# A post-norm decoder layer on one core: the self-attention scores in 64-row tiles, queries masked four ways out of PSUM, and every engine's order laid anew

## The chip, the core and the metric

The kernel runs on one core of a Trainium2 chip. A core has a matrix engine (TensorE, PE in the profile; its weight loads are PEld), a vector engine (VectorE, DVE), a scalar engine (ScalarE, ACT), GpSimd (POOL) and SyncE (SP), whose queue issues the DMAs. The engines run their own instruction streams in order and meet at semaphores. SBUF is the on-chip memory of 128 partitions. PSUM takes TensorE's results; here it is cut into six banks B0 to B5 of 512 columns and a double one, S.

The metric is the time of one execution on the device, in microseconds. The kernel before took 1192.78 us (median of three runs, 1187.5 to 1199.39).

## The reference, cut to what matters

128 sequences of 64 tokens, 128 features. Each of three blocks is followed by a residual sum and a layer norm.

```python
# 1: causal self-attention, 16 heads of 8; no softmax but a polynomial
att = einsum('bhid,bhjd->bhij', q, k) / sqrt(8), causal
p   = polymax(att)          # x > 0: x**2 + 1;  -100 <= x <= 0: 1 - x/100;  else 0;  all / 1000
x   = layernorm(x + (p @ v) @ W_proj)
# 2: cross-attention over 64 context rows, 16 heads of 64, softmax
x   = layernorm(x + softmax(q @ k.T / 8) @ v @ WO + bO)
# 3: 16 experts, the top 6 of a softmax router, gates normalised
x   = layernorm(x + sum_e gate_e * (x @ expert_w[e]) / sum(gate))
```

All in float32. Where the kernel multiplies with the faster float32r form, it splits a number into a high and a low part and adds three products (hi.hi, hi.lo, lo.hi): `mm3` in the code.

## The kernel before, in words

A tile is four sequences (`NB`), 256 tokens; there are 32 tiles. One **turn** of the main loop works on five tiles at once, a stage on each: `s1` (self-attention scores, tile i+2), `l1` (the rest of self-attention, and the context products Z and VB, tile i+1), `l2` (cross-attention, router logits, tile i), `ff` (gates and experts, tile i-1), `out` (last norm and store, tile i-2). There is one turn for each of the 32 tiles besides a few that fill and empty the pipeline; 30 or so run with all stages on.

What sets the order is written out in tables: `JOBS` is TensorE's order with the PSUM bank of each job, and `SP_ORDER`, `ACT_ORDER`, `DVE_ORDER`, `POOL_ORDER` are those of the other engines. Each word names a function (`row_max0` is `row_max(0)`). A job waits until its bank's last job was emptied.

The steps that the change and the prediction touch:

- **Q and K** (TensorE): 128x256 products into one bank each. Keys: ScalarE writes `kp_hi` (`move_keys`), VectorE `kp_lo` (`keys_lo0`, `keys_lo1`), masked two ways (even and odd heads). Queries: ScalarE moves Q to `q_sb` (step `Q`), GpSimd splits it (`q_hi`, `q_lo`), ScalarE masks the high part eight ways (`queries_hi0` and `queries_hi1`, four copies each, into `qm_hi`), VectorE the low part in one instruction of 2048 columns (L820, `queries_lo`).
- **S1_0 to S1_3** (TensorE): for a sequence, 128 contraction rows, 512 query columns (8 masks x 64 tokens), three products, one bank.
- **Polymax**: for each S1 bank ScalarE does `relu` and `square`, VectorE `allow` (L730), `pieces` (L736) and `p1_` (L741). Of these only `p1_` has both inputs in SBUF (`poly` and `allowed`).
- **Cross-attention**: S2 -> `row_max`, `less_max` (VectorE) -> `exp` (ScalarE) -> `row_sum`, `row_inv` (VectorE) -> `shares` (GpSimd, L890, 128x1024) -> the transposes PT -> AC.
- **Layer norms** 1, 2, 3 (`stats`, `var`, `eps` on VectorE, `root` on GpSimd, L885, `norm` on VectorE, L698, two instructions each with SBUF input and output).
- **Gates**: `gate0` to `gate19`, twenty small VectorE steps in a chain. **Experts**: FF0 to FF7 -> `weigh0` to `weigh7` (VectorE, L754) -> `add0.0` to `add1.4` (GpSimd, L904 and L909; the first of each five is 128x1024).
- **SyncE**: loads, the store, and `place0`, `place1`: four DMAs each of 256 KB that move `vb_raw` to `vb` (L352).

Of the kernel before, what the change touches and what calls it, by code (L numbers as in the profile page):

```python
# [1010 lines left out]
```

## Time and profile before

| | value |
|---|---|
| median of three runs | 1192.78 us |
| lowest, highest run | 1187.5, 1199.39 us |
| profiled execution, first to last instruction (its own time is not printed beside it) | 1184.6 us |
| busy: PE, DVE, ACT, POOL | 95%, 94%, 65%, 62% |
| granted TensorE clock, mean | 0.990 of full speed |
| DMA, mean | 78 GB/s; queue q1 30.7% of 16 engines |
| chain that ended last | PE 46%, DVE 33%, issue 17% |

Busy time is the union of an engine's records. A record of VectorE runs some tens of ns into the next one, so the time that an instruction takes of its engine is read from start to start. Matmul records overlap more: their starts, not their lengths, say how fast TensorE goes. A record's length includes the time in which an instruction that has started is held up.

### The profile page before, as it was taken

The numbers are of one execution on the slowest core, as the hardware profiler recorded it, in microseconds if no ns is written. First come the engines' busy times: TensorE is split into PE (matmuls) and PEld (weight loads), VectorE is DVE, ScalarE is ACT, GpSimd is POOL, SyncE is SP. The second block draws the span as 40 slices with busy tenths as digits, with TensorE's granted clock in tenths as the row PEclk, the third lists the DMA queues.
The fourth block names the chain that finished last, engine by engine and source line by source line (L and its number), as shares of the span: only waits on it lengthen the run. The fifth ranks groups of instructions, "written<-read, shape, count | busy, mean of one in ns | idle before, by whom it ended". The sixth has DMA issues, their size and how long they took to land.

```text
span 1184.6 us, 30898 instructions
## 1 busy us (share of the span) xinstructions
PE 1126.7 (95%) x9472; PEld 867.1 (73%) x9472; DVE 1112.7 (94%) x2699; ACT 770.0 (65%) x1578; POOL 736.9 (62%) x776
## 2 busy tenths in 40 slices
...
DMA packets 49998, 92.09 MB, mean 78 GB/s; under 512 B 6576, under 2 KB 28592, under 8 KB 49968
## 3 DMA queue, kind: packets, MB, share of 16 engines
q1 hardware_dynamic: 49968, 91.70, 30.7%
...
## 4 chain that ended last, share of the span: by engine, by line
PE 46%; DVE 33%; issue 17%; DVEq 1%; POOL 1%; ACT 1%; DMA 1%; SPq 0%; POOLq 0%
PE ps_B L368 36%; DVE weighted L754 7%; PE ps_S L368 5%; PE ps_B L476 5%; DVE x L698 5%; DVE p L741 3%; DVE allowed L730 3%; DVE rowmax L709 3%; DVE kp_lo L826 2%; DVE poly L736 2%; DVE stats L676 2%; DVE r L839 1%; DVE mv L682 1%; DVEq L246 1%; DVE rowsum L718 0%
## 5 line engine op out<-in xcount | busy, mean ns | idle before, releaser
L904 POOL TENSOR_TENSOR weighted<-weighted 128x1024 f32<-128x1024 f32 (+3 forms) x256 | 313.3, 1224 | 103.5 <-DVE weighted L754 100.5
L890 POOL TENSOR_TENSOR p<-p,rowinv 128x1024 f32<-128x1024 f32 x64 | 122.9, 1920 | 194.3 <-DVE rowinv L722 194.3
L542 ACT ACTIVATE z<-ps_B 128x512 f32<-128x512 f32 x256 | 149.7, 599 | 118.2 <-PE ps_B L368 115.3
L754 DVE TENSOR_TENSOR weighted<-ps_B,gate 128x512 f32<-128x512 f32 x256 | 171.8, 684 | 14.7 <-PE ps_B L368 9.5
L368 PE MATMUL ps_B<-cT_hi,a_hi 128*128 128x256 f32 x512 | 156.0, 305 | 1.5
L698 DVE TENSOR_SCALAR x<-r,mv,rstd 128x128 f32<-128x128 f32 x192 | 152.5, 835 | 2.9 <-POOL rstd L885 2.9
L542 ACT ACTIVATE vb_raw<-ps_B 128x512 f32<-128x512 f32 x256 | 147.4, 590 | 5.4 <-PE ps_B L368 3.0
L368 PE MATMUL ps_B<-cT_hi,a_lo 128*128 128x256 f32 x512 | 144.6, 282 | 0.0
L368 PE MATMUL ps_B<-cT_lo,a_hi 128*128 128x256 f32 x512 | 144.6, 282 | 0.0
L368 PE MATMUL ps_B<-vo_hi,cT_hi 128*128 128x512 f32 x256 | 112.7, 440 | 16.4 <-DVE kp_lo L826 10.5
L368 PEld LDWEIGHTS ps_B<-vb,p2T 128*64 128x64 f32 x2048 | 110.6, 137 | 23.4 <-issue 23.2
L368 PE MATMUL ps_S<-z,x1T 128*64 128x512 f32 x512 | 124.0, 605 | 2.6 <-DVE p L713 2.6
L368 PE MATMUL ps_B<-vb,p2T 128*64 128x128 f32 x2048 | 126.0, 276 | 0.0
L542 ACT ACTIVATE p2T<-ps_B 128x512 f32<-128x512 f32 x128 | 69.6, 595 | 75.1 <-PE ps_B L476 75.1
L885 POOL TENSOR_TENSOR rstd<-rstd,power 128x2 f32<-128x2 f32 x96 | 67.0, 708 | 82.2 <-DVE rstd L686 81.9
L368 PE MATMUL ps_B<-ex_hi,x2T_hi 128*128 128x512 f32 x256 | 110.5, 432 | 5.9 <-DVE weighted L754 3.6
L368 PEld LDWEIGHTS ps_B<-cT_hi,a_hi 128*128 128x128 f32 x512 | 97.1, 190 | 21.9 <-DVE r L839 13.9
L542 ACT ACTIVATE qm_hi<-q_hi,const 128x256 fp32r<-128x256 f32 x256 | 108.9, 499 | 5.7 <-POOL q_hi L932 5.5
L368 PE MATMUL ps_B<-ex_lo,x2T_hi 128*128 128x512 f32 x256 | 101.7, 397 | 0.0
L368 PE MATMUL ps_B<-ex_hi,x2T_lo 128*128 128x512 f32 x256 | 101.6, 397 | 0.0
L368 PE MATMUL ps_B<-vo_lo,cT_hi 128*128 128x512 f32 x256 | 100.7, 394 | 0.0
L730 DVE SCALAR_TENSOR_TENSOR allowed<-ps_B,const 128x512 f32<-128x512 f32 x128 | 87.0, 679 | 14.6 <-ACT relu L566 14.5
...
## 6 DMA issues: line engine op xcount, KB each, us to landing
vb<-vb_raw SPq DMA_DIRECT2D x256, 256.0 KB, 4.3
...
```

Of the source, the lines that this page charges most:

```text
L368: return pe.matmul(o, l, r, start=start, stop=stop)
L476: last = pe.transpose(ps[BANK[f"PT{r}" + "ab"[q]]][:, P * k:P * k + P], p2[:, r, P * j:P * j + P], ident)
L542: return nc.scalar.activation(dst, src, ACT.Copy, scale=scale)
L676: V.bn_stats(stats[:, n - 1, r], src[:, r]).then_inc(ln_stats[n - 1], 1)
L698: V.tensor_scalar(dst[:, r], src[:, r], mv[:, n - 1, r, 0:1], rstd[:, n - 1, r:r + 1], ALU.subtract, ALU.mult).then_inc(done, 1)
L709: V.tensor_reduce(rowmax[:, r], ps["S"][:].rearrange("p (h k) -> p h k", h=H), AX.X, ALU.max).then_inc(rowmax_ready, 1)
L730: V.scalar_tensor_tensor(allowed[:].rearrange("p (j n) -> p j n", j=J), ps[BANK[f"S1_{b}"]][:].rearrange("p (j n) -> p j n", j=J), -100.0, ...
L741: V.scalar_tensor_tensor(p1[:, b], poly[:], 1.0, allowed[:], ALU.add, ALU.mult).then_inc(p1_ready, 1)
L754: V.tensor_tensor(weighted[:, r, 512 * q:512 * q + 512].rearrange("p (e c) -> p e c", e=4), ps[BANK[job]][:].rearrange("p (e c) -> p e c", ...
L885: G.tensor_tensor(rstd[:, n - 1], rstd[:, n - 1], power[:], ALU.pow).then_inc(ln_rstd[n - 1], 1)
L890: G.tensor_tensor(weights, weights, rowinv[:, r].unsqueeze(2).broadcast_to([P, H, T]), ALU.mult).then_inc(p2_ready, 1)
L904: G.tensor_tensor(a, a, b, ALU.add).then_inc(add_steps, 1)
```

## The change

1. **Scores in two 64-row tiles.** Queries are masked four ways rather than eight (`NV = 4`), each mask keeping the heads of one 16-row group in either half of the partitions. A product takes 64 rows of keys (rows 0 to 63 or 64 to 127) against 256 query columns, and two such go to two banks, one after the other in the instruction stream. An S1 bank now holds four head pairs of two sequences instead of eight of one; S1_0 is issued with S1_1, S1_2 with S1_3, at the later one's place. `p1_` writes two blocks of 256 columns.
2. **Queries out of PSUM.** ScalarE writes `qm_hi` straight from Q's bank in four masked copies (`queries_hi`; the scale is in `query_mask`), VectorE writes `qm_lo` in four instructions of 256 columns from the same bank. Gone are the move to `q_sb`, GpSimd's `q_hi` and `q_lo`, four masked copies on ScalarE and the 2048-column instruction on VectorE.
3. **Orders.** All five tables are new. The setup products stand at their ends.

```diff
+PARTS = 2
+NV = J // PARTS
+PART = P // PARTS
...
 SP_ORDER = """
-    x_columns place0 store context x_rows place1
+    context x_rows x_columns store place0 place1
...
+    gate18 allow3 pieces3 attended gate19 stats2 weigh1 var2 weigh0 eps2 weigh3 weigh2 norm2 weigh7 weigh5 weigh4
+    logits p1_3 gate0 weigh6 gate1 product_lo0 product_lo1 product_lo2 product_lo3 product_lo4 product_lo5
...
+    context_hi context_lo add1.0 add1.1 add1.2 add1.3 add1.4 shares0 next_x_hi root3 shares1 root1 next_x_lo bias_x1
+    root2 add0.0 add0.1 x2_hi add0.2 x2_lo add0.3 add0.4 experts_hi experts_lo
...
+def latest(jobs, waited=()):
+
+    order = [job for job, _, _ in JOBS]
+    return [job for job in jobs if BANK[job] not in waited and job == last_of(order, [other for other in jobs if BANK[other] == BANK[job]])]
...
-                def s1(b):
-                    pe.wait_ge(qm_hi_ready, 2 * (u + 1))
-                    pe.wait_ge(qm_lo_ready, u + 1)
-                    wait_emptied(pe, i, "K")
-                    k_hi, k_lo = (a[:, b].rearrange("p a t -> p (a t)") for a in (kp_hi, kp_lo))
-                    q_hi, q_lo = (a[:, b].rearrange("p j t -> p (j t)") for a in (qm_hi, qm_lo))
-                    return mm3(ps[BANK[f"S1_{b}"]][:], k_hi, k_lo, q_hi, q_lo)
+                def s1(last_unit):
+                    units = range(last_unit - PARTS + 1, last_unit + 1)
+                    for job in latest(("Q", "K"), [BANK[f"S1_{unit}"] for unit in units]):
+                        wait_emptied(pe, i, job)
+                    seqs = range(NB * units[0] // 4, NB * (last_unit + 1) // 4)
+                    for s, b in enumerate(seqs):
+                        for n, (keys, queries) in enumerate(((kp_hi, qm_hi), (kp_hi, qm_lo), (kp_lo, qm_hi))):
+                            for g, unit in enumerate(units):
+                                rows = slice(PART * g, PART * g + PART)
+                                done = mm(ps[BANK[f"S1_{unit}"]][:, NV * T * s:NV * T * s + NV * T], keys[rows, b].rearrange("p a t -> p (a t)"),
+                                          queries[rows, b].rearrange("p v t -> p (v t)"), n == 0, n == 2)
...
-                def move_q():
-                    move("Q", q_sb[:], ps[BANK["Q"]][:, 0:TOK], float(HD) ** -0.5)
-
-                def queries_hi(half):
-
-                    act.wait_ge(q_hi_ready, u + 1)
-                    for j in range(4 * half, 4 * half + 4):
-                        last = copy(qm_hi[:, :, j], q_hi[:].rearrange("p (b t) -> p b t", b=NB), qmask[:, j:j + 1])
+                def queries_hi():
+
+                    wait_full(act, i, "Q")
+                    for v in range(NV):
+                        last = copy(qm_hi[:, :, v], ps[BANK["Q"]][:, 0:TOK].rearrange("p (b t) -> p b t", b=NB), query_mask[:, v:v + 1])
...
                 def p1_of(b):
...
-                    V.scalar_tensor_tensor(p1[:, b], poly[:], 1.0, allowed[:], ALU.add, ALU.mult).then_inc(p1_ready, 1)
+                    seqs, heads = slice(b // 2 * 2, b // 2 * 2 + 2), slice(b % 2 * NV * T, b % 2 * NV * T + NV * T)
+                    V.scalar_tensor_tensor(p1[:, seqs, heads], poly[:].rearrange("p (s n) -> p s n", s=2), 1.0, allowed[:].rearrange("p (s n) -> p s n", s=2), ALU.add, ALU.mult).then_inc(p1_ready, 1)
...
                 def queries_lo():
...
-                    dve.wait_ge(q_lo_ready, u + 1)
-                    V.tensor_tensor(qm_lo[:], q_lo[:].rearrange("p (b t) -> p b t", b=NB).unsqueeze(2).broadcast_to([P, NB, J, T]),
-                                    qmask.unsqueeze(1).unsqueeze(3).broadcast_to([P, NB, J, T]), ALU.mult).then_inc(qm_lo_ready, 1)
+                    dve.wait_ge(qm_hi_ready, u + 1)
+                    if isinstance(i, int) and u == 0:
+                        dve.wait_ge(mask_steps, 2)
+                    for v in range(NV):
+                        last = V.scalar_tensor_tensor(qm_lo[:, :, v], ps[BANK["Q"]][:, 0:TOK].rearrange("p (b t) -> p b t", b=NB), query_mask[:, v:v + 1],
+                                                      qm_hi[:, :, v].bitcast(F32), ALU.mult, ALU.subtract)
+                    last.then_inc(emptied[BANK["Q"]], 1)
...
-                def queries_hi():
-                    wait_emptied(pool, i, "Q")
-                    G.tensor_tensor(q_hi[:].bitcast(F32R), q_sb[:], one[:].broadcast_to([P, TOK]), ALU.mult).then_inc(q_hi_ready, 1)
-
-                def queries_lo():
-                    pool.wait_ge(q_hi_ready, u + 1)
-                    G.tensor_tensor(q_lo[:], q_sb[:], q_hi[:], ALU.subtract).then_inc(q_lo_ready, 1)
```

Three places of the new order, as the instruction streams have them. The first is VectorE in the loop, around the reciprocal `rowinv` of sequences 2 and 3 (`row_inv1`), which lets GpSimd start `shares1`. Before:

```order
L246 REGISTER_ALU [waits allowed_ready]
L741 SCALAR_TENSOR_TENSOR p1<-poly,allowed 128x512 [waits emptied_B1]
L722 RECIPROCAL rowinv<-rowsum 128x16 [waits rowsum_ready]
L763 REGISTER_ALU
L794 TENSOR_SCALAR tsum<-tsum 128x2 [waits gate_steps]
L763 REGISTER_ALU
L796 TENSOR_TENSOR gate<-prob,left 128x32 [waits gate_steps]
L679 REGISTER_ALU
L661 MEMSET scratch 128x1 [waits ln1_stats]
L682 BN_AGGR mv<-stats 128x2 x2
L729 REGISTER_ALU [waits p1_ready]
L730 SCALAR_TENSOR_TENSOR allowed<-ps_B4,const 128x512 [waits relu_ready]
```

And now:

```order
L812 TENSOR_TENSOR gate<-prob,left 128x32 [waits gate_steps]
L737 RECIPROCAL rowinv<-rowsum 128x16 [waits rowsum_ready]
L779 REGISTER_ALU
L814 RECIPROCAL tinv<-tsum 128x2 [waits gate_steps]
L252 ISA [waits allowed_ready]
L757 SCALAR_TENSOR_TENSOR p1<-poly,allowed 128x2x256 [waits emptied_B2]
L779 REGISTER_ALU
L816 TENSOR_TENSOR gate<-gate,tinv 128x32 [waits gate_steps]
L701 TENSOR_SCALAR rstd<-mv 128x2 [waits ln1_var]
L779 REGISTER_ALU
L818 TENSOR_REDUCE gsum<-gate 128x2 [waits gate_steps]
L252 ISA
```

Behind `rowinv` stood a small gate step, the statistics of a norm and `allowed`, which reads PSUM; now `p1` (two SBUF inputs), a gate product and the sum of norm 1 (`rstd<-mv`) stand there, and norms 3 and 1 follow within a few rows.

The second is GpSimd at the same place. Before:

```order
L888 REGISTER_ALU
L890 TENSOR_TENSOR p2<-p2,rowinv 128x1024 [waits rowinv_ready]
L870 TENSOR_TENSOR xT_lo<-xT,xT_hi 128x256 [waits xT_hi_ready]
L900 REGISTER_ALU
L904 TENSOR_TENSOR weighted<-weighted 128x128 [waits add_steps]
L885 TENSOR_TENSOR rstd<-rstd,power 128x2 [waits ln1_eps]
```

And now:

```order
L905 TENSOR_TENSOR rstd<-rstd,power 128x2 [waits ln3_eps]
L908 REGISTER_ALU
L910 TENSOR_TENSOR p2<-p2,rowinv 128x1024 [waits rowinv_ready]
L905 TENSOR_TENSOR rstd<-rstd,power 128x2 [waits ln1_eps]
L890 TENSOR_TENSOR xT_lo<-xT,xT_hi 128x256 [waits xT_hi_ready]
L969 REGISTER_ALU
L252 ISA [waits x1_ready]
```

`shares1` (`p2<-p2,rowinv`) now has norm 1's root and the split of the next x directly behind it.

The third is TensorE at S1_2 and S1_3. Before, S1_2 is three products of 512 columns into one bank, between Z and AC1:

```order
L368 MATMUL ps_B5<-cT_hi,a_hi 128x256
L368 MATMUL ps_B5<-cT_lo,a_hi 128x256
L368 MATMUL ps_B5<-cT_hi,a_lo 128x256
L246 REGISTER_ALU
L368 MATMUL ps_B3<-qm_hi,kp_hi 128x512
L368 MATMUL ps_B3<-qm_lo,kp_hi 128x512
L368 MATMUL ps_B3<-qm_hi,kp_lo 128x512
```

And now both are twelve products of 256 columns, by turns into B3 and B2:

```order
L374 MATMUL ps_B3<-qm_hi,kp_hi 128x256
L374 MATMUL ps_B2<-qm_hi,kp_hi 128x256
L374 MATMUL ps_B3<-qm_lo,kp_hi 128x256
L374 MATMUL ps_B2<-qm_lo,kp_hi 128x256
L374 MATMUL ps_B3<-qm_hi,kp_lo 128x256
L374 MATMUL ps_B2<-qm_hi,kp_lo 128x256
L374 MATMUL ps_B3<-qm_hi,kp_hi 128x256
L374 MATMUL ps_B2<-qm_hi,kp_hi 128x256
L374 MATMUL ps_B3<-qm_lo,kp_hi 128x256
L374 MATMUL ps_B2<-qm_lo,kp_hi 128x256
L374 MATMUL ps_B3<-qm_hi,kp_lo 128x256
L374 MATMUL ps_B2<-qm_hi,kp_lo 128x256
```

The first of each two reads rows 0 to 63, the second rows 64 to 127.

## Rows read from the trace of the kernel before

**Rows 1.** The page, busy time of each engine: us (share of span) xinstructions.
```profile
PE 1126.7 (95%) x9472; PEld 867.1 (73%) x9472; DVE 1112.7 (94%) x2699; ACT 770.0 (65%) x1578; POOL 736.9 (62%) x776
```

**Rows 2.** Busy time in a stretch of 700 us: PE, PEld, DVE, ACT, POOL, clock, DMA.
```profile
395.00:1095.00 700.00, 686.01 (x5856) 526.47 (x5854) 681.85 (x1667) 474.00 (x974) 449.56 (x473) 1.00 0.31 77
```

**Rows 3.** One line each over its executions in that stretch: duration ns min/median/max.
```profile
L820 DVE TENSOR_TENSOR qm_lo<-q_lo,const x20: 2664/3142/3361, 402.4 to 1072.7; 128x2048 fp32r<-128x2048 f32 x20
...
L741 DVE SCALAR_TENSOR_TENSOR p<-poly,allowed x80: 678/681/1117, 394.9 to 1089.8; 128x512 f32<-128x512 f32 x80
...
L698 DVE TENSOR_SCALAR x<-r,mv,rstd x192: 333/349/2405, 47.7 to 1182.0; 128x128 f32<-128x128 f32 x192
```

**Rows 4.** Groups by form, whole span: busy us, mean ns of one | idle before.
```profile
L820 DVE TENSOR_TENSOR qm_lo<-q_lo,const 128x2048 fp32r<-128x2048 f32 x32 | 93.2, 2913 | 0.0
...
L826 DVE SCALAR_TENSOR_TENSOR kp_lo<-ps_B,const,kp_hi 128x256 fp32r<-128x256 f32 x64 | 28.0, 478 | 4.6 <-ACT kp_hi L542 4.6
...
L698 DVE TENSOR_SCALAR x<-r,mv,rstd 128x128 f32<-128x128 f32 x192 | 152.5, 835 | 2.9 <-POOL rstd L885 2.9
...
L542 ACT ACTIVATE qm_hi<-q_hi,const 128x256 fp32r<-128x256 f32 x256 | 108.9, 499 | 5.7 <-POOL q_hi L932 5.5
...
L936 POOL TENSOR_TENSOR q_lo<-q_sb,q_hi 128x256 f32<-128x256 f32 x32 | 23.5, 733 | 2.5
...
L904 POOL TENSOR_TENSOR weighted<-weighted 128x1024 f32<-128x1024 f32 x64 | 152.4, 2381 | 100.5 <-DVE weighted L754 100.5
...
L890 POOL TENSOR_TENSOR p<-p,rowinv 128x1024 f32<-128x1024 f32 x64 | 122.9, 1920 | 194.3 <-DVE rowinv L722 194.3
...
L885 POOL TENSOR_TENSOR rstd<-rstd,power 128x2 f32<-128x2 f32 x96 | 67.0, 708 | 82.2 <-DVE rstd L686 81.9
```

**Rows 5.** Timeline, one turn, TensorE: start us, us, instruction.
```profile
614.79 0.40 PE L368 MATMUL ps_B<-vo_lo,cT_hi 128*128 128x512 f32 x1
...
615.02 0.40 PE L368 MATMUL ps_B<-vo_hi,cT_lo 128*128 128x512 f32 x1
...
615.35 1.94 PE L368 MATMUL ps_S<-z,x1T 128*64 128x512 f32 x8
...
618.70 0.28 PE L368 MATMUL ps_B<-cT_hi,a_hi 128*128 128x256 f32 x1
...
618.82 0.28 PE L368 MATMUL ps_B<-cT_lo,a_hi 128*128 128x256 f32 x1
```

**Rows 6.** Timeline, GpSimd, then VectorE: a norm behind an expert addition.
```profile
632.83 2.37 POOL L904 TENSOR_TENSOR weighted<-weighted 128x1024 f32<-128x1024 f32 x1 [2.84 <-DVE weighted L754]
...
633.35 2.19 DVE L698 TENSOR_SCALAR x<-r,mv,rstd 128x128 f32<-128x128 f32 x2
...
635.46 0.68 DVE L730 SCALAR_TENSOR_TENSOR allowed<-ps_B,const 128x512 f32<-128x512 f32 x1
```

**Rows 7.** Timeline of the setup, GpSimd, then VectorE: `p1` behind `ex_lo`.
```profile
22.57 4.54 POOL L945 TENSOR_TENSOR ex_lo<-p2T,ex_hi 128x2048 fp32r<-128x2048 f32 x1
...
25.17 2.49 DVE L741 SCALAR_TENSOR_TENSOR p<-poly,allowed 128x512 f32<-128x512 f32 x1
```

**Rows 8.** Timeline, VectorE, then GpSimd: what stands behind `rowinv` of sequences 2, 3.
```profile
625.54 0.25 DVE L722 RECIPROCAL rowinv<-rowsum 128x16 f32<-128x16 f32 x1
...
625.84 0.19 DVE L796 TENSOR_TENSOR gate<-prob,left 128x32 f32<-128x32 f32 x1
...
626.15 0.68 DVE L730 SCALAR_TENSOR_TENSOR allowed<-ps_B,const 128x512 f32<-128x512 f32 x1
...
627.99 0.53 DVE L686 TENSOR_SCALAR rstd<-mv 128x2 f32<-128x2 f32 x1
...
625.86 1.94 POOL L890 TENSOR_TENSOR p<-p,rowinv 128x1024 f32<-128x1024 f32 x1 [2.33 <-DVE rowinv L722]
...
627.76 0.72 POOL L870 TENSOR_TENSOR xT_lo<-xT,xT_hi 128x256 fp32r<-128x256 f32 x1
```

**Rows 9.** Timeline, SyncE's queue: four moves of `vb`.
```profile
599.15 3.14 SPq L352 DMA_DIRECT2D vb<-vb_raw  x4
```

More of the change, by code:

```diff
@@ L78 @@
 SP_ORDER = """
-    x_columns place0 store context x_rows place1
+    context x_rows x_columns store place0 place1
 """.split()
 ACT_ORDER = """
-    Q K queries_hi0 VB0 exp0 Y queries_hi1 VB1 V VB3 product_hi0 VB4 relu0 Z7 square0 Z1 exp1 Z5 VB2 PT0a
-    PT0b relu1 product_hi1 product_hi2 square1 Z2 VB7 PT1b product_hi3 PT1a Z4 relu2 square2 product_hi4 Z3
-    Z0 base3 Z6 X1T relu3 product_hi5 X2T square3 VB6 product_hi6 VB5 logit_exp product_hi7
+    K queries_hi exp0 Y VB3 VB1 VB7 V Z2 VB5 VB2 relu0 square0 VB4 relu1 Z1 square1 exp1 Z6 Z3 PT0a VB6 PT0b Z0 Z4
@@ L85 @@
+    PT1b relu2 square2 PT1a relu3 Z7 square3 base3 X1T Z5 X2T VB0 logit_exp product_hi0 product_hi1 product_hi2
+    product_hi3 product_hi4 product_hi5 product_hi6 product_hi7
 """.split()
 DVE_ORDER = """
-    row_max0 less_max0 gate2 gate3 keys_lo0 keys_lo1 queries_lo row_sum0 gate4 row_inv0 row_max1 gate5
-    less_max1 allow0 gate6 projected gate7 gate8 pieces0 product_lo0 product_lo1 stats1 gate9 gate10
-    row_sum1 p1_0 row_inv1 product_lo2 gate11 gate12 var1 allow1 pieces1 gate13 gate14 gate15 eps1 gate16
@@ L90 @@
-    gate17 gate18 gate19 weigh1 product_lo3 weigh0 weigh3 p1_1 weigh2 stats3 var3 norm1 allow2 product_lo4
-    attended stats2 eps3 var2 eps2 weigh6 pieces2 norm2 weigh7 norm3 p1_2 product_lo5 weigh4 allow3 pieces3
-    logits gate0 p1_3 product_lo6 product_lo7 gate1 weigh5
+    row_max0 gate2 less_max0 gate3 keys_lo0 gate4 keys_lo1 queries_lo row_sum0 row_max1 gate5 projected gate6
+    less_max1 gate7 stats1 gate8 row_inv0 var1 gate9 stats3 gate10 allow0 pieces0 var3 p1_0 allow1 pieces1 gate11
@@ L93 @@
+    eps3 row_sum1 gate12 row_inv1 gate13 p1_1 gate14 eps1 gate15 norm3 gate16 norm1 allow2 pieces2 gate17 p1_2
+    gate18 allow3 pieces3 attended gate19 stats2 weigh1 var2 weigh0 eps2 weigh3 weigh2 norm2 weigh7 weigh5 weigh4
+    logits p1_3 gate0 weigh6 gate1 product_lo0 product_lo1 product_lo2 product_lo3 product_lo4 product_lo5
+    product_lo6 product_lo7
 """.split()
 POOL_ORDER = """
-    context_hi context_lo q_hi q_lo add1.0 shares0 add1.1 add1.2 experts_hi next_x_hi shares1 next_x_lo
@@ L96 @@
-    add1.3 root1 add1.4 add0.0 root2 experts_lo root3 add0.1 bias_x1 add0.2 x2_hi add0.3 x2_lo add0.4
+    context_hi context_lo add1.0 add1.1 add1.2 add1.3 add1.4 shares0 next_x_hi root3 shares1 root1 next_x_lo bias_x1
+    root2 add0.0 add0.1 x2_hi add0.2 x2_lo add0.3 add0.4 experts_hi experts_lo
 """.split()
@@ L175, in decoder @@
         cT_hi, cT_lo = sb("cT_hi", [P, TOK], F32R), sb("cT_lo", [P, TOK], F32R)
-        q_sb = sb("q_sb", [P, TOK])
-        q_hi, q_lo = sb("q_hi", [P, TOK]), sb("q_lo", [P, TOK])
-        qm_hi, qm_lo = sb("qm_hi", [P, NB, J, T], F32R), sb("qm_lo", [P, NB, J, T], F32R)
+        head_mask, query_mask = sb("head_mask", [P, NV]), sb("query_mask", [P, NV])
+        qm_hi, qm_lo = sb("qm_hi", [P, NB, NV, T], F32R), sb("qm_lo", [P, NB, NV, T], F32R)
         kp_hi, kp_lo = sb("kp_hi", [P, NB, 2, T], F32R), sb("kp_lo", [P, NB, 2, T], F32R)
```

20 lines of the change are left out of this document (13 added, 7 removed), and 24 rows, old and new, of the table JOBS.

## The prediction

> **What bounds the kernel now.** I read the page's busy times first: TensorE 95%, VectorE 94%, the others near 62 to 65% [rows 1]. Two engines that close need a steady stretch. In 700 us from 395 to 1095, VectorE is busy 681.85 us and TensorE 686.01 [rows 2]. A line that runs once a turn has 20 executions there (the first of rows 3), so a turn is 35.0 us, VectorE works 34.1 of it and is idle 0.9. TensorE's 34.3 flatters it: a matmul record of 512 columns is 0.40 us long, but the next starts 0.23 us later, and 256 columns take 0.12 from start to start [rows 5]. VectorE bounds the turn.
>
> What fills VectorE is the next view. `x<-r,mv,rstd` (the norms) has a median of 0.349 us and a mean of 0.835, with 2.405 at most [rows 3, 4]. The timeline says why: GpSimd's 128x1024 addition starts at 632.83 and ends at 635.20, a pair of norm instructions starts at 633.35 and ends at 635.54, a third of a microsecond after GpSimd's end [rows 6]. `p1` does the same in the setup: it starts at 25.17 and takes 2.49 us rather than 0.68, ending 0.55 after GpSimd's `ex_lo` [rows 3, 7]. And `rstd<-mv` takes 0.53 us while GpSimd splits x [rows 8]. Each of these VectorE instructions has all its inputs in SBUF; `allowed`, which reads PSUM, keeps its 0.68 us beside a running GpSimd instruction [rows 8]. So **a VectorE instruction with two SBUF tensors, or one that copies SBUF to SBUF with scalars, stands until GpSimd's running instruction has ended.** I call that time held. By this trace it is of the size of what the change removes, and the new orders move all of it.
>
> The Trainium skill, "SBUF — State Buffer", section "SBUF: two separate sides", says it as a rule: the port pair that VectorE and GpSimd share is an exclusive lock for a whole instruction, and the other fully blocks. By that rule, the trace agrees [rows 6, 7], held time is laid anew with the order, and the sum is the one below; were it a fixed tax that no order moves, the sum would be 35.0 - 1.4 = 33.6 a turn, 1151 us.
>
> **The change, a turn at a time, on VectorE.**
>
> *Queries.* The 2048-column instruction goes: median 3.14 us [rows 3], part of it held. Four of 256 columns come, from PSUM, like `kp_lo`: 28.0 us for 64, 0.44 each [rows 4], 1.75 together. That reads PSUM and cannot be held. **-1.4.** `p1_` writes the same 512 columns in two blocks: 0.
>
> *Held time that goes.* The norms take 152.5 us [rows 4], 4.8 a turn, for three pairs; two free ones of 0.35 are 0.6, so 1.8 is work and 3.0 held. Of the small ones `rstd<-mv` loses about 0.4 of its 0.53 (an estimate, by GpSimd's end at 628.48). Together **-3.4.** The new order decides anew about all of these.
>
> *Held time that comes.* Four places, each walked with the durations of rows 4.
>
> (a) Behind `row_inv1`. The order rows show `tinv`, then `p1_1`, `gate14`, the sum of norm 1 (`eps1`), `gate15`, norm 3, `gate16`, norm 1. GpSimd starts `shares1` 0.3 us after `rowinv` starts (625.54, 625.86 [rows 8]), before `p1_1` can go, and holds for 1.92. Then `p1_1` 0.6, `gate14` and `eps1` 0.3; only then has GpSimd its root of norm 1, 0.7, and right behind it the low split of x, 0.72. Norm 3 meets the one and the other, norm 1 follows, another 0.9 for both ends. Sum 1.9 + 0.6 + 0.3 + 0.7 + 0.7 + 0.9 and the gates, about 5.4, for 2.4 of work: **+3.0.** Were `p1_1` first, `shares1` would only start later and hold `gate14` instead. Before, the instructions behind this `rowinv` read PSUM or were short: nothing was held. Bounds: 2.2 (norm 3 slips in before the root) to 3.4.
>
> (b) Norm 2 stands directly behind `weigh2`, whose end is what `add0.0` waits for. The first of the pair may get in, the second waits 2.38: **+2.2**, as at 633.35 [rows 6]. Bounds 1.8 to 2.5.
>
> (c) `p1_3` and `gate1` stand among the weighings where GpSimd does `x2_hi`, `add0.2`, `x2_lo`, `add0.3`, `add0.4`, each 0.4 to 0.8 us long, almost without a gap. One or both are held: 0 to 1.4, I take **+0.6**, a little below the middle, since I can't place them to a tenth of a microsecond.
>
> (d) `gate4` (`prob<-logit,linv`) stands between the two `kp_lo`. GpSimd then has done the context's split and begins `add1.0`, 2.38 us long. By my walk VectorE arrives at its end; earlier by 2 us it would be held for all. 0 to 2.4, **+0.4**, near the walk's 0.6.
>
> Together **+6.2**, between 4.0 and 9.7.
>
> *Idle.* VectorE's 0.9 a turn of waiting shrinks when it is later and the others are not: with ScalarE relieved (below) and TensorE shorter, I take 0.3. **-0.6.** Bounds: -0.9 to 0.
>
> Sum: 35.0 - 1.4 - 3.4 + 6.2 - 0.6 = **35.8 us, 0.8 more a turn**.
>
> **The other engines.** *TensorE*: S1 is 12 products of 512 columns now, 12 x 0.23 = 2.8 us. It becomes 12 pairs of 256. Pairs of output tiles do run together here: S2's eight records of 512 columns take 1.94 us [rows 5]. Nothing shows pairs of row tiles. Together they take 12 x 0.12 = 1.4, one by one 24 x 0.12 = 2.9; the switch of tile form costs up to 0.1 each way (0.33 from 615.02 to 615.35, rather than 0.23 [rows 5]). So -1.2 to +0.4, at 34.3 busy of 35.8: no cost, VectorE's work covers it. If that cover went, a turn could not be below about 33.0 or, one by one, 34.6. *ScalarE* loses the move of Q and four of eight masked copies at 0.43 (108.9 / 256 [rows 4]), 2 us of a 65% busy engine: no gain but the idle term. *GpSimd* loses `q_hi` and `q_lo`, 0.7 each [rows 4]; it waits for VectorE anyway. *SyncE*: `place0` and `place1` now follow one another behind `VB0`, late in the turn, eight DMAs at 3.14 us for four [rows 9], so their data is under way for some 10 us and `VB7`'s eviction on ScalarE waits for the second four. Behind it in ScalarE's order stand `V`, `Z2`, `VB5`, `VB2`, `relu0`. VectorE needs `relu0` some 11 us into the turn; ScalarE gets there a microsecond or more ahead: 0, and if the moves are slower than now, up to +1. *Setup and drain*: the products come after the scores rather than among them, 0, with 3 us either way.
>
> **The numbers.** Some 30 turns are of this kind: 30 x 0.8 = 24 us. The profiled execution spans 1184.6; the median of the runs is 8.2 above it, and I keep that distance. 1184.6 + 24 + 8.2 = **1217 us.**
>
> **Rivals.**
>
> *A. Faster: the waits fall between GpSimd's instructions.* Held time then is 4.2 rather than 6.2: `p1_3`, `gate1`, `gate4` run free, and in (a) norm 3 gets in before the root. For it: such positions hang on tenths of a microsecond, and on VectorE bare work falls by 1.4. Against it: (a) and (b) follow from the order itself, since one engine's next instruction is released by what the other has just ended. Idle time would shrink less, by 0.3: 35.0 - 1.4 - 3.4 + 4.2 - 0.3 = 34.1, 30 x 0.9 = 27 less, **1166**. It decides when held time is under about 5.4. If held time stays even at today's 3.4 and idle as it is, 1.4 x 30 = 42 less: 1151. Chance 0.27.
>
> *B. No change.* Held time near 5.4: (a) and (b) as walked, (c) and (d) nothing. 35.0 a turn, **1193**. Chance 0.22.
>
> *C. The row tiles do not run together.* Nothing in my forecast moves; in A the turn becomes 34.6 and the time 1181. For it: no row shows them at once. It is a part of A's and B's chance, 0.05.
>
> Forecast: 0.51. A measurement of this kernel can tell about 1% from no change (its runs spread by 1%). Faster by over 1% is A, 0.27; within 1% is B, 0.22; slower by over 1% is the forecast, 0.51. The range: 1155, where A is nearly whole, to 1250, where (c) or (d) costs a microsecond more than I took (35.8 + 1.1, 30 x 1.9 = 57). The forecast's own range is 1205 to 1250.
>
> **What would show it.** Right: a turn near 35.8; `qm_lo` four times near 0.44; `p1`'s mean well over 0.68, with one in four near 2 us and ending with GpSimd's `p<-p,rowinv`; norm 2 near 2.7 for the pair; VectorE busy 98 to 99%. S1 pairs 0.12 apart show the tiles at once. Wrong: `p1` at its 0.68 throughout, or norms of under 4 us a turn; then A. Wrong in another way: VectorE idle 1 us or more a turn before `allowed` or `r<-ps_B,x1b`; then TensorE or ScalarE sets the turn, through a chain that I took as covered.

## The result, and the profile after

The changed kernel takes 1231.1 us (median of 4 runs, 1230.7 to 1231.4), the kernel before in the same comparison 1193.0 (1187.5 to 1199.4). The ratio is 1.031, 95% interval 1.025 to 1.037: **slower**. The forecast was 1217, with 0.51 on this side.

The profiled execution spans 1228.9 us, 44.3 more than before. (The medians differ by 38.1 only: the profiled execution of the kernel before was a fast one among its runs.) The row that runs once a turn on VectorE, `r<-ps_B,x1b`, comes every 35.97 us in the middle of the program (mean of 15 turns), every 35.29 before. Where the 44.3 lie, from the starts of the row maximum of sequence pair 0, which comes once a turn, 32 times:

| stretch of the profiled execution | before, us | changed, us | difference |
|---|---|---|---|
| ahead of the first | 53.59 | 55.78 | 2.2 |
| first to second | 28.15 | 35.17 | 7.0 |
| the 29 full turns behind it, each | 35.29 | 35.99 | 29 x 0.70 = 20.3 |
| the last but one to the last | 28.57 | 34.17 | 5.6 |
| behind the last | 51.0 | 60.2 | 9.2 |

In the 29 every stage is on (but for `out` in the first of them). Less than half of the loss is in these full turns; the filling and the emptying of the pipeline lost 24.0 us.

The stretch of [rows 2], columns as there:

```profile
395.00:1095.00 700.00, 669.92 (x5950) 514.58 (x5949) 680.84 (x1689) 419.64 (x855) 426.25 (x426) 1.00 0.31 75
```

The stretch holds 700 / 35.97 = 19.46 turns: VectorE is busy 35.0 us a turn and idle 1.0. Before, with 700 / 35.29 = 19.84 turns, it was 34.4 and 0.9: its idle time did not shrink. What did change is the chain that ended last. The page gave TensorE 46%, VectorE 33%, "issue" 17% and DMA 1% before; now:

```profile
PE 61%; DMA 13%; DVE 11%; SPq 6%; issue 5%; ACT 3%; POOL 2%; DVEq 0%; ACTq 0%; POOLq 0%
```

A fifth of the span is now a transfer and the issuing of it. One turn of that chain, in order of time (start us, us, what):

```profile
597.88 5.05 DMA vb<-vb_raw
...
603.04 0.60 ACT vb_raw L556
...
603.88 5.71 PE ps_B L374 x42
...
616.06 4.54 PE ps_B L374 x67
...
620.82 2.12 PE ps_B L374 x9
...
623.83 2.42 DVE x L713
...
626.30 0.44 PE ps_B L504 x2
...
629.89 1.97 PE ps_B L374 x70
631.86 0.16 SPq L358
...
633.86 5.05 DMA vb<-vb_raw
```

It is a ring: the last of the `place` DMAs, the eviction of `VB7`, TensorE back to back for 19 us, norm 2 on VectorE, `X2T`, and, by way of `VB0`'s eviction, the DMAs again. The chain steps from TensorE to SyncE's queue at 631.86, but the queue has been issuing since 627.72: it starts behind `VB0`'s eviction, which stands behind `X2T`'s in ScalarE's order. SyncE's row in the timeline shows both places in one piece, where [rows 9] had four at a time:

```profile
627.05 0.59 ACT L556 ACTIVATE vb_raw<-ps_B 128x512 f32<-128x512 f32 x1
...
627.72 7.32 SPq L358 DMA_DIRECT2D vb<-vb_raw  x8
```

How TensorE comes to wait for `VB7`'s eviction is in the code: `S1_0` takes `VB7`'s bank, B5. Its products are issued with `S1_1`'s, but its wait for the bank has stayed at its own place in the order, ahead of `VB2`, so it is `VB2` that starts late (603.88). Moving that wait was not tried.

What TensorE and the `VB7` eviction wait for, 395 to 1095 us (engine line <- whom: us in total, times, longest):

```profile
ACT vb_raw L556 <- DMA vb<-vb_raw: 25.7, 19, 1.5
...
PE ps_B L504 <- DVE x L713: 11.5, 20, 0.6
PE ps_B L374 <- DVE kp_lo L846: 9.2, 19, 0.5
PE ps_B L374 <- ACT vb_raw L556: 4.5, 15, 0.4
```

Most of TensorE's idle time (700 less 669.92, 30.1 us) stands there: 0.6 us a turn for norm 2, 0.5 for `kp_lo` (behind the held `gate4`), 0.2 for `VB7`.

The DMAs weigh more in the first turn, where ScalarE's eviction waits 2.64 us for them (SyncE, then ScalarE):

```profile
54.17 7.42 SPq L358 DMA_DIRECT2D vb<-vb_raw  x8
...
66.24 0.60 ACT L556 ACTIVATE vb_raw<-ps_B 128x512 f32<-128x512 f32 x1 [2.64 <-DMA vb<-vb_raw]
```

From 50 to 70 us TensorE is busy 15.87 us there; in the kernel before it is busy all 20.

The held instructions were where the prediction put them. VectorE's timeline (start us, us, instruction), of `gate14` behind `shares1`, of norm 2 and of `gate4` inside `add1.0`:

```profile
611.55 0.69 DVE L757 SCALAR_TENSOR_TENSOR p<-poly,allowed 128x512 f32<-128x512 f32 x1
612.16 1.89 DVE L816 TENSOR_TENSOR gate<-gate,tinv 128x32 f32<-128x32 f32 x1
...
623.58 2.67 DVE L713 TENSOR_SCALAR x<-r,mv,rstd 128x128 f32<-128x128 f32 x2
...
633.25 1.66 DVE L797 TENSOR_TENSOR prob<-logit,linv 128x32 f32<-128x32 f32 x1
```

and GpSimd's beside them:

```profile
611.65 2.35 POOL L910 TENSOR_TENSOR p<-p,rowinv 128x1024 f32<-128x1024 f32 x1 [0.74 <-DVE rowinv L737]
...
623.74 3.79 POOL L924 TENSOR_TENSOR weighted<-weighted 128x1024 f32<-128x1024 f32 x2 [0.62 <-DVE weighted L770]
...
632.50 3.73 POOL L924 TENSOR_TENSOR weighted<-weighted 128x1024 f32<-128x1024 f32 x2
```

The row tiles run together: TensorE's pairs start 0.12 us apart, and one S1 call, to the start of the next product, takes 605.65 - 604.74 = 0.91 us.

```profile
604.42 0.40 PE L374 MATMUL ps_B<-vo_hi,cT_lo 128*128 128x512 f32 x1
...
604.74 0.39 PE L374 MATMUL ps_B<-qm_hi,kp_hi 64*128 64x256 f32 x2
604.97 0.28 PE L374 MATMUL ps_B<-qm_lo,kp_hi 64*128 64x256 f32 x2
605.08 0.28 PE L374 MATMUL ps_B<-qm_hi,kp_lo 64*128 64x256 f32 x2
...
605.65 0.50 PE L374 MATMUL ps_B<-vo_hi,cT_hi 128*128 128x512 f32 x1
...
605.99 0.39 PE L374 MATMUL ps_B<-vo_lo,cT_hi 128*128 128x512 f32 x1
```

Around the call two starts are further apart than the 0.23 us of such products: 0.32 ahead of it (from 604.42), 0.34 behind it (to 605.99). With that, a call costs 0.91 + 0.09 + 0.11 = 1.1 us, 2.2 a turn. Before, a call of three products, half as much, took 0.69 us, from here to the start at 618.70 of [rows 5], 2.8 a turn:

```profile
618.01 0.40 PE L368 MATMUL ps_B<-qm_hi,kp_hi 128*128 128x512 f32 x1
```

So the scores got about 0.5 us a turn shorter on TensorE.

### The profile page after: what moved, and what is told of

Its sections match the earlier page's. It is cut to its first block, busy times and chain, and to the rows that moved or that the text cites. A ratio compares the mean times of both kernels' runs of the same rounds, so it can differ in the third digit from the quotient of the medians.

```text
span 1228.9 us, 31448 instructions
## 1 busy us (share of the span) xinstructions
PE 1124.1 (91%) x9856; PEld 862.3 (70%) x9856; DVE 1130.2 (92%) x2797; ACT 699.5 (57%) x1418; POOL 710.4 (58%) x712
## 4 chain that ended last, share of the span: by engine, by line
PE 61%; DMA 13%; DVE 11%; SPq 6%; issue 5%; ACT 3%; POOL 2%; DVEq 0%; ACTq 0%; POOLq 0%
PE ps_B L374 49%; DMA vb<-vb_raw 12%; DVE x L713 6%; SPq L358 5%; PE ps_B L488 5%; PE ps_S L374 5%; ACT vb_raw L556 2%; POOL weighted L924 2%; DVE weighted L770 1%; PE ps_B L504 1%; DVE allowed L745 1%; PE ps_B L457 1%; DVE p L757 0%; DVE poly L751 0%; ACT z L556 0%
## 5 line engine op out<-in xcount | busy, mean ns | idle before, releaser
L924 POOL TENSOR_TENSOR weighted<-weighted 128x1024 f32<-128x1024 f32 (+3 forms) x256 | 311.6, 1217 | 33.5 <-DVE weighted L770 23.3
L910 POOL TENSOR_TENSOR p<-p,rowinv 128x1024 f32<-128x1024 f32 x64 | 135.0, 2109 | 151.5 <-DVE rowinv L737 151.5
L713 DVE TENSOR_SCALAR x<-r,mv,rstd 128x128 f32<-128x128 f32 x192 | 132.3, 730 | 6.7 <-POOL rstd L905 4.1
L374 PE MATMUL ps_B<-vb,p2T 128*64 128x128 f32 x2048 | 121.2, 277 | 0.0
L374 PEld LDWEIGHTS ps_B<-vb,p2T 128*64 128x64 f32 x2048 | 113.4, 139 | 5.5 <-issue 5.5
L757 DVE SCALAR_TENSOR_TENSOR p<-poly,allowed 128x512 f32<-128x512 f32 x128 | 109.8, 858 | 1.2
L972 POOL TENSOR_TENSOR x1b<-x,bo_sb 128x256 f32<-128x256 f32 x32 | 23.6, 736 | 147.8 <-DVE r L859 147.3
L556 ACT ACTIVATE x2T<-ps_B 128x256 f32<-128x256 f32 x32 | 12.3, 385 | 165.3 <-PE ps_B L504 165.3
```

Source lines behind the costliest of these rows:

```text
L374: return pe.matmul(o, l, r, start=start, stop=stop)
L556: return nc.scalar.activation(dst, src, ACT.Copy, scale=scale)
L713: V.tensor_scalar(dst[:, r], src[:, r], mv[:, n - 1, r, 0:1], rstd[:, n - 1, r:r + 1], ALU.subtract, ALU.mult).then_inc(done, 1)
L757: V.scalar_tensor_tensor(p1[:, seqs, heads], poly[:].rearrange("p (s n) -> p s n", s=2), 1.0, allowed[:].rearrange("p (s n) -> p s n", s=2 ...
L910: G.tensor_tensor(weights, weights, rowinv[:, r].unsqueeze(2).broadcast_to([P, H, T]), ALU.mult).then_inc(p2_ready, 1)
L924: G.tensor_tensor(a, a, b, ALU.add).then_inc(add_steps, 1)
```

## The experiments

Two theories stood against each other. **T1**, the prediction's: VectorE's time, held time in it, sets the turn, so each hold that goes gives its length back. **T2**, read from the trace after: the ring above sets it, and a hold counts only where it lies in the ring. Kernels e1 to e4 ran in one comparison on one chip, e5 to e8 in a second, e9 to e12 in a third, each beside the kernel before (1193.0, 1189.2 and 1189.8 us); across them the ratios and the turns of the traces are what is compared. The turn is the mean of 15 in the middle. Line numbers of a variant are shifted by what it adds.

| kernel | us | ratio to before, 95% | turn us |
|---|---|---|---|
| before | | | 35.29 |
| changed | 1231.1 | 1.025 to 1.037 | 35.97 |
| e1 gate4 | 1230.9 | 1.029 to 1.034 | 35.97 |
| e2 norm2 | 1210.1 | 1.011 to 1.016 | 35.19 |
| e3 place1 | 1224.0 | 1.024 to 1.029 | 35.91 |
| e9 gate4, place1 | 1194.7 | 1.003 to 1.007 | 34.86 |
| e4 all three | 1180.3 | 0.987 to 0.994 | 34.39 |
| e6 and p1_3 | 1169.2 | 0.980 to 0.984 | 33.96 |
| e8 and drain order | 1167.1 | 0.979 to 0.983 | 33.98 |
| e5 e4, tiles in series | 1193.8 | 1.002 to 1.006 | 34.73 |
| e10 e4, same rows | 1221.6 | 1.023 to 1.028 | 35.55 |
| e7 e4, old queries | 1280.8 | 1.073 to 1.078 | 37.73 |
| e11 before, +1.21 us VectorE | 1235.0 | 1.034 to 1.039 | 36.92 |
| e12 e6, +1.21 us VectorE | 1174.4 | 0.985 to 0.990 | 34.16 |

**e1: one hold taken away.**

```
- keys_lo0 gate4 keys_lo1 queries_lo row_sum0 row_max1 gate5 projected
+ keys_lo0 keys_lo1 queries_lo row_sum0 row_max1 gate4 projected gate5
```

> The changed kernel with gate4 (prob = logit x linv, 128x32, held for 1.66 us inside add1.0) issued behind row_max1, when GpSimd's additions are over; nothing else moves. T1, VectorE's held time sets the turn: its 1.4 us a turn come back, 36.0 -> 34.6 us, about 1187 us. T2, the turn is set by a ring norm 2 -> X2T -> VB0's eviction -> the eight DMAs of place -> VB7's eviction -> TensorE, and gate4's hold lies beside it: TensorE's wait for kp_lo (0.48 us a turn) goes and its wait for VB7 grows by as much; 36.0 us stays, 1226 to 1232 us.

1230.9 us. VectorE's busy time in the stretch fell from 680.8 to 655.9 us, 1.3 us a turn, and the turn did not move. T1 falls. The waits show T2's exchange: `kp_lo` is gone from TensorE's waits, and `VB7` took it over.

```profile
ACT vb_raw L556 <- DMA vb<-vb_raw: 36.8, 19, 2.0
...
PE ps_B L374 <- ACT vb_raw L556: 16.5, 19, 0.9
```

**e2: the hold inside the ring taken away.**

```
- weigh3 weigh2 norm2 weigh7
+ weigh3 norm2 weigh2 weigh7
```

> The changed kernel with norm2 issued one weigh earlier (eps2 weigh3 norm2 weigh2), so that it runs before add0.0 starts on GpSimd; nothing else moves. T1: the hold of 2.0 us a turn comes back, 36.0 -> 34.0 us, about 1170 us. T2: X2T follows FF5 without TensorE's idle 0.58 us, and the ring is shorter by that alone, since TensorE stands between: 36.0 -> 35.4 us, about 1212 us.

1210.1 us, 0.78 us a turn: T2's figure within 2 us, T1's 40 off. The 2 us of hold were worth the 0.6 that TensorE had waited and a little more. The ring is still there: in the page's chain DMA has 13% and SyncE's queue 6%, as without the edit.

**e3: place1 before place0.**

```
- x_columns store place0 place1
+ x_columns store place1 place0
```

> The changed kernel with place1 issued before place0 on SP's queue; nothing else moves. T1: VectorE's path has no DMA in it: 36.0 us stays, 1231 us. T2: place1 is issued behind AC1 at about 620 instead of 631 us, VB7's eviction no longer waits for its DMAs (1.41 us idle on ScalarE a turn goes), and TensorE's idle 0.33 us before VB2 goes: 36.0 -> 35.5 to 35.7 us, 1214 to 1222 us; what is late next is kp_lo behind gate4's hold.

1224.0 us, a little slower than T2 allowed, and only 0.06 us a turn in the middle, where T2 had 0.3 to 0.5: T2 as it stands misses, too. Of the 7.1 us of span that the edit brings, 4.2 are in the first turn (35.17 to 30.95), where the DMAs had stood in TensorE's way, and 3.2 in the 29 full ones. The wait for the DMAs is gone, as expected; `kp_lo` kept TensorE waiting as before, and the chain of the page is TensorE 42%, VectorE 34%, "issue" 19%, DMA 0%. This suggests a third theory, **T3**: a chain through VectorE is level with the ring, and each edit opens only one of the two.

```profile
PE ps_B L504 <- DVE x L713: 11.6, 20, 0.6
PE ps_B L374 <- DVE kp_lo L846: 9.3, 19, 0.5
PE ps_B L374 <- DVE poly L751: 4.2, 19, 0.3
```

**e4: the three together.** Diff as in e1, e2 and e3.

> The three edits together: gate4 behind row_max1, norm2 before weigh2, place1 before place0. T1: 1.4 + 2.0 us a turn, 36.0 -> 32.6 us until TensorE bounds it (34.5 us busy a turn): about 1185 us. T2: TensorE's idle of 1.4 us a turn (0.48 + 0.33 + 0.58) goes, 36.0 -> 34.6 us, about 1187 us. The two agree on this one; it shows what is left when neither the holds nor the ring is in the way, and what VectorE does with the time.

1180.3 us, below both kernels. The waits show one place where TensorE still idles, 0.5 us a turn, S2_1 behind `less_max0`:

```profile
PE ps_S L374 <- DVE p L728: 10.0, 21, 2.4
```

The three edits gave 0.00, 0.78 and 0.06 us a turn one by one, and 1.58 together.

**e9: the two that gave next to nothing a turn, together.** This tests T3. Diff as in e1 and e3.

> The changed kernel with gate4 behind row_max1 and place1 before place0, norm2 left where it is. Alone the first edit gave 0.0 us a turn and the second 0.06. T3, two chains are level, one through the place DMAs and one through VectorE with its held time, and each edit opens only one of them: together they give more than their sum, 36.0 -> 35.0 us a turn, about 1195 to 1205 us, with X2T's wait for norm 2 (0.58 us) left. If the two add up (T2 as it was): 35.9 us, 1222 to 1226 us. T1: 34.6 us, 1185 us.

1194.7 us, 1.11 us a turn for two edits that gave 0.06 in sum (e9 ran in a later comparison; by ratios 1.005 against 1.032 and 1.026). T3 holds: the time is just below its range on a chip where the kernel before is 3 us faster, and the turn is 0.1 below the forecast one. That the two add up is out. TensorE's wait for `kp_lo` and for `VB7` are both gone; norm 2's is left:

```profile
PE ps_B L504 <- DVE x L713: 12.2, 21, 0.7
```

So `gate4`'s hold was worth about 1.05 us a turn and nothing, by what stood beside it.

**e6: the last wait.**

```
- weigh3 norm2 weigh2 weigh7 weigh5 weigh4 logits p1_3 gate0
+ weigh3 p1_3 norm2 weigh2 weigh7 weigh5 weigh4 logits gate0
```

> The kernel of the three edits (e4) with p1_3 issued between weigh3 and norm2, before GpSimd's additions, instead of behind logits, where it is held (1.40 us for 0.69). In e4 TensorE's only idle time in the turn is 0.38 us before S2_1, which waits for less_max0 on VectorE. T2, TensorE bounds the turn and gives back its idle time alone: 34.39 -> 34.0 us, about 1168 us. T1, VectorE's held time counts (0.7 us back): 33.7 us, about 1158 us. If norm2's delay of 0.35 us is passed on to X2T: 1180 us as before.

1169.2 us, with 1168 expected: 1.8% faster than the kernel before. `less_max0` no longer keeps TensorE waiting in the stretch but once, and TensorE is busy 695.63 us of the 700 of [rows 2]:

```profile
395.00:1095.00 700.00, 695.63 (x6315) 544.27 (x6313) 644.75 (x1788) 451.03 (x904) 442.74 (x454) 1.00 0.33 80
```

**e11 and e12: the same dose on VectorE in two kernels.** The prediction began with "VectorE bounds the turn"; this tests it in the kernel before, and its contrary in e6. The dose's input tile is set once, in the setup.

```
+ if b == 2:   # behind p1_2
+     V.tensor_reduce(dose_out[:], dose_in[:].rearrange("p (h k) -> p h k", h=H), AX.X, ALU.add)
```

> The kernel before with one more reduction on VectorE a turn, 128x16<-128x1024 from a constant tile in SBUF, 1.21 us, behind p1_2; its result is used by nobody. The prediction's premise, VectorE bounds the turn of before: +1.2 us a turn, 31 x 1.2 = +37 us, 1225 to 1231 us. If TensorE or a chain beside VectorE is level with it (34.3 us of TensorE busy in a turn of 35.3): +0.9 to 1.2 us all the same. If VectorE has slack there: under +10 us.

> The kernel of e6 (gate4, norm2, place1 and p1_3 moved) with the same added reduction of 1.21 us behind p1_2. TensorE bounds this kernel (695.6 of 700 us busy, VectorE 644.8): the 1.2 us go into VectorE's idle time of 2.7 us a turn, +0 to +0.3 us a turn, 1169 to 1180 us. If VectorE's time still counts: +37 us, 1206 us.

Before: 1235.0 us, 1.63 us a turn for 1.21 of work, more than expected. Held time came with the dose: `p1`, four a turn, now takes 0.794 us on average in the stretch, 0.693 without it, which is 0.4 us a turn. VectorE had no slack there. That it bounded the turn alone is not shown: a chain level with it would have given nearly the same, as the expectation says. TensorE's waits for `poly` and `kp_lo` grew (from 0.5 and 7.6 us):

```profile
PE ps_B L370 <- DVE poly L740: 23.3, 19, 1.4
PE ps_B L370 <- DVE kp_lo L832: 12.7, 19, 0.7
```

In e6: 1174.4 us, 0.20 us a turn; where the 0.20 come from I did not follow. TensorE is as busy as without the dose. VectorE took most of it into its idle time, which fell from 2.7 to 1.9 us a turn:

```profile
395.00:1095.00 700.00, 695.63 (x6265) 539.71 (x6262) 660.32 (x1802) 447.08 (x897) 441.99 (x454) 1.00 0.33 80
```

**e5 and e10: what the two row tiles are worth.**

```
e5:
- for s, b in enumerate(seqs): for n, ...: for g, unit in enumerate(units):
+ for g, unit in enumerate(units): for s, b in enumerate(seqs): for n, ...:
e10:
- rows = slice(PART * g, PART * g + PART)
+ rows = slice(0, PART)
```

> The kernel of the three edits (e4) with the S1 pair's matmuls in another order: all six of the first 64-row tile, then all six of the second, so that no two neighbours lie on different rows; the same 12 matmuls of 256 columns, same banks, same places. If the two tiles run at the same time (pairs start 0.12 us apart, one pair of calls takes 0.91 us), in series it takes 12 x 0.12 + 0.2 = 1.6 us, +0.7 a pair and +1.4 us a turn on TensorE, which bounds e4: 34.4 -> 35.4 to 35.8 us, 1212 to 1224 us. If tiles on different rows are served one after the other anyway (rival), nothing changes: 1180 us.

> The kernel of e4 with both units of an S1 pair reading rows 0 to 63 (the second unit's heads are left out, the first unit's are computed twice); the same 12 matmuls of 64 rows and 256 columns in the same order into the same two banks. If in e4 neighbours on different rows run at the same time, they can't here: 12 x 0.12 + 0.2 = 1.6 us a pair instead of 0.91, +1.4 us a turn on TensorE, which bounds this kernel: 34.4 -> 35.4 to 35.8 us, 1212 to 1224 us. In e5 (in series) the trace shows the second tile's first three matmuls beside the first tile's last three, 1.25 us a pair, and 34.7 us a turn. If the row tile makes no difference (rival): 34.4 us, 1180 us.

e5 missed its expectation: 1193.8 us, 0.34 us a turn instead of 1.0 to 1.4. Its trace says why: issued one tile behind the other, they still overlap by half.

```profile
621.38 0.27 PE L374 MATMUL ps_B<-qm_hi,kp_lo 64*128 64x256 f32 x1
621.38 0.38 PE L374 MATMUL ps_B<-qm_hi,kp_hi 64*128 64x256 f32 x2
621.61 0.28 PE L374 MATMUL ps_B<-qm_lo,kp_hi 64*128 64x256 f32 x2
...
622.29 0.50 PE L374 MATMUL ps_B<-vo_hi,cT_hi 128*128 128x512 f32 x1
```

The second tile's first products stand beside the first tile's last three; the call, from 621.04, takes 1.25 us, not 1.6. e10 (it leaves out the second unit's heads) shuts that out, and has 1221.6 us, as expected (it ran later than e4; ratios 1.026 and 0.991). Its pairs start 0.23 apart from the second on, and a call takes 1.60 us:

```profile
603.21 0.50 PE L374 MATMUL ps_B<-qm_hi,kp_hi 64*128 64x256 f32 x2
603.55 0.39 PE L374 MATMUL ps_B<-qm_lo,kp_hi 64*128 64x256 f32 x2
603.77 0.40 PE L374 MATMUL ps_B<-qm_hi,kp_lo 64*128 64x256 f32 x2
...
604.81 0.50 PE L374 MATMUL ps_B<-vo_hi,cT_hi 128*128 128x512 f32 x1
```

That the two tiles run at once thus saves 2 x 0.69 us of TensorE a turn, of which 1.16 show in the turn where TensorE bounds it. That is against the same 64-row products one by one; against the 128-row products of the kernel before the change saves about 0.5 us, as the rows above show. The Trainium skill, "TensorEngine Tiling (Array Packing)", section "Key Properties", says that different tiles can load and multiply in parallel; by that page, the trace agrees for two 64-row tiles into two banks.

**e7: the queries' old path.**

```
- copy(qm_hi[:, :, v], ps[BANK["Q"]]..., query_mask[:, v:v + 1])                  # ScalarE, 4 times
- V.scalar_tensor_tensor(qm_lo[:, :, v], ps[BANK["Q"]]..., query_mask..., qm_hi...)  # VectorE, 4 times
+ move("Q", q_sb[:], ps[BANK["Q"]][:, 0:TOK], float(HD) ** -0.5)                  # ScalarE
+ q_hi = q_sb * one;  q_lo = q_sb - q_hi                                          # GpSimd
+ copy(qm_hi[:, :, v], q_hi..., head_mask[:, v:v + 1])                            # ScalarE, 4 times
+ V.tensor_tensor(qm_lo[:], q_lo..., head_mask..., ALU.mult)                      # VectorE, once
```

The lines are shortened. In the orders, ScalarE has `Q K exp0 Y queries_hi` for `K queries_hi exp0 Y`, and GpSimd has `q_hi q_lo` ahead of `add1.0`.

> The kernel of the three edits (e4) with the queries' old path under the new two-tile layout: ScalarE copies Q to SBUF with the scale, GpSimd makes the high and the low part (2 x about 0.65 us ahead of add1.0), ScalarE masks the high part four ways from SBUF, VectorE masks the low part in one instruction of 128x1024 with both inputs in SBUF. VectorE's own time falls from 1.65 to about 1.1 us, but GpSimd starts add1.0 right behind the low part, and the instruction may be held up to 2.3 us. TensorE bounds this kernel, and VectorE has some 2.4 us a turn to spare: T2 says 1178 to 1190 us, the part on the queries is worth nothing or up to 10 us here. T1 (VectorE's time counts): +0.5 to 1.8 us a turn, 1195 to 1235 us.

1280.8 us, 3.34 us a turn more than e4 (its turns vary, by 37.7 to 38.0 for 15 of them), far outside both theories' ranges. The hold I had allowed (2.3 us) came, but behind a wait for GpSimd's `q_lo` that I had not counted. VectorE:

```profile
621.05 3.41 DVE L845 TENSOR_TENSOR qm_lo<-q_lo,head_mask 128x1024 fp32r<-128x1024 f32 x1 [1.33 <-POOL q_lo L961]
```

GpSimd, whose additions `add1` start beside it:

```profile
620.98 5.96 POOL L929 TENSOR_TENSOR weighted<-weighted 128x1024 f32<-128x1024 f32 x4
```

TensorE's product behind `PR`'s bank, emptied by `projected`, which stands behind `qm_lo` on VectorE:

```profile
627.37 0.50 PE L376 MATMUL ps_B<-vo_hi,cT_hi 128*128 128x512 f32 x1 [2.36 <-DVE r L858]
```

TensorE waits 44.9 us in the stretch for `projected`, 2.4 a turn and most of the 3.34. VectorE had time to spare over the turn, but none between Q and `projected`. Reading the queries from PSUM takes both the wait and the hold away. How much it is worth in other orders was not tried; this order was laid for the new path.

**e8: the drain.** e6, with one turn's order changed on TensorE.

```
+ if isinstance(i, int) and i == NT - 1:   # early: FF1, FF0, FF2, FF6
+     jobs[at:at] = early                    # at: the place of PT0a
```

> The kernel of e6 with another order on TensorE in one turn, the last that has the attention stage: FF1, FF0, FF2 and FF6 are issued ahead of PT0a instead of behind AC1; all other turns are as in e6. In the profile of the changed kernel TensorE idles 5.4 us before PT0a there, the granted clock is 0.51 in 1180 to 1190 us, the transposes take 1.1 instead of 0.6 us for four and the 64 matmuls of AC 6.03 instead of 3.71 us. If that is what the drain lost: last row_max1 to the end 55 -> 50 to 52 us, 3 to 5 us less than e6. If the drain is bound by GpSimd's additions alone (rival): as e6 within 1 us.

1167.1 against 1169.2 us, spans 1164.3 against 1167.5, intervals that overlap: not settled by the times. In the traces the products of AC took 4.66 instead of 6.15 us. TensorE in e6, in that turn:

```profile
1116.48 1.09 PE L488 MATMUL ps_B<-const,p 128*128 128x128 f32 x4 [5.62 <-POOL p L910]
...
1122.81 6.15 PE L374 MATMUL ps_B<-vb,p2T 128*64 128x128 f32 x64
```

and in e8:

```profile
1114.89 0.63 PE L488 MATMUL ps_B<-const,p 128*128 128x128 f32 x4 [2.63 <-POOL p L916]
...
1121.22 4.66 PE L374 MATMUL ps_B<-vb,p2T 128*64 128x128 f32 x64
```

From `S2_1` to the end e8 has 57.0 us and e6 58.6 (from 1107.33 and 1108.91), so the edit brought 1.6 us in the drain, less than the 3 to 5 expected. The other 1.6 arose earlier. `PT0a` comes 7.6 us behind `S2_1` in both: it waits for GpSimd's `shares0`, and the four transposes, two to a bank, wait for each other's evictions (0.69 us each). That share of the drain is seen in the traces only.

## Why the prediction was right, and where it was not

The direction and the place in the range were right. The mechanism was right in part: held time came about as foretold, but VectorE's time does not set the turn by itself, and the largest part of what was missed is outside the full turns. The closeness of the turn (+0.70 for +0.8) is in good part luck: VectorE's busy time rose by 0.6 where 1.4 was forecast, its idle time by 0.1 where -0.6 was.

*The turn before, 35.0.* It was 35.29: 20 starts of a row in 700 us are 19 turns and a remainder, and from 402.4 to 1072.7 [rows 3] the 19 take 35.28 each. The difference of two turns is not touched by it.

*Queries, -1.4.* Right: four `qm_lo` in 1.64 us for 3.03 on average (60.5 us for 20).

*Held time that comes, +6.2.* Right in sum, with two misses that cancel, from the rows of one turn: `gate14` 1.7 and norm 1 0.3 behind `row_inv1`, where I had +3.0 (`p1_1` got in ahead of `shares1`, the case I had named, and norm 3 ran free), 2.0 in all and below the bound of 2.2; norm 2 2.1, with 2.2 foretold; `p1_3` and `gate1` 0.8 for 0.6; `gate4` 1.5 for 0.4, within its bounds. 6.4 in all. With -1.4 and -3.4 VectorE should be busier by 1.6 us a turn; it is by 0.6 (34.4 to 35.0). About half of the other microsecond is held time of before that the -3.4 left out: `logit<-logit,lmax` took 0.372 us on average, `gate<-gate,tinv` 0.320 and the first `gsum` step 0.304, where each is free in under 0.2. The rest I did not follow.

*Idle, -0.6.* Wrong. VectorE waits 1.0 us a turn as before (0.9). The prediction had named this as the sign of a chain taken as covered.

*"VectorE bounds the turn."* For the kernel before, e11 bears it out so far that VectorE had no slack; for the kernel after it is wrong: there e1 took 1.3 us a turn off VectorE for nothing. Two chains were level.

*SyncE, "0, up to +1".* **In the turn, this is the step that failed**, with the rule behind it that VectorE's terms may be added up. I had seen the eight DMAs in one piece and `VB7`'s eviction waiting for them, and priced it by the slack of `relu0` on VectorE. The one who waits for `VB7`'s bank is TensorE, ahead of `VB2`, and from there the ring closes over norm 2. Taken away by itself it is worth 0.06 us a turn (e3); its price shows only beside the others, and the sum of the turn hides it: the hold of norm 2 counted for 0.78 us instead of 2.0, `gate4`'s for nothing, and the DMAs kept both from showing.

*TensorE, "no cost, covered".* Wrong in the same way: it stands in the ring for most of the turn (61% of the chain). The saving was priced too high as well: -1.2 at best was allowed for S1 with the switch of form, and the rows show about -0.5 (2.2 for 2.8 us). The floor of 33.0 for a turn that TensorE bounds is not reached either: e6, where TensorE is busy 99.4% of the stretch, has 33.96. In the kernel after the saving was used up by the waits.

*Setup and drain, 0 with 3 either way.* **In the time, this is the term that was furthest off**: +24.0 us, 9.2 ahead of the full turns (2.2 and 7.0) and 14.8 behind them (5.6 and 9.2). Of the first 7.0, e3 gives back 4.2: there the price of the eight DMAs is plain. In the drain all of FF stands behind AC, so TensorE idles 5.4 us ahead of `PT0a`, and behind that the granted clock is 0.51 from 1180 to 1190 us, the lower of its two levels (1.2 GHz): AC takes 6.03 us there, 3.71 in the steady turn. The kernel before had FF products between PT and AC, and a clock of 0.83 from 1140 to 1150. e8 gives back 1.6 us of this. The rest stays open, the 5.6 of the last turn with it (e3, with the DMAs early, has 34.3 us there as well), and nothing was tried on the setup as such.

*The sum.* 30 x 0.8 = 24 was forecast for the turns, 20.3 came; 0 for the ends, 24.0 came; and the median of after lies 2.2 us above the profiled span, not 8.2. 1184.6 + 20.3 + 24.0 + 2.2 = 1231.1. The 14 us between forecast and result are the ends, less the 6.0 of the median and the 3.7 of the turns.

*The signs.* `qm_lo` (0.47), norm 2 (2.67 for the pair) and the tiles' starts came as named. `p1` did not: its mean is 0.82 us in the stretch, and none is over 1.25, since the held one behind `rowinv` was `gate14`. VectorE was busy 97.3%, not 98 to 99, and idle 1.0 us a turn, 0.7 of it before `allowed` and `r<-ps_B,x1b`: the sign named for a chain taken as covered.

*The rivals.* A needed held time under 5.4: it was 6.4. C is out by e10. Where the expected gain of the change went: with three steps of the order put elsewhere (e4) the same operations make the turn 0.90 us shorter than before, and with a fourth (e6) 1.33. So the instructions could have made a faster turn, and the order they came in cost 1.58 to 2.0 us of it.
